# Row maxima of two attention layers: products on 32-row groups of the array, and the row of maxima written by transfer

## Reference

```python
x = x + tanh(g_xattn[0]) * attention0(layernorm(x), ctx, mask)   # 16 heads of 8
x = x + tanh(g_ffn[0])   * moe0(layernorm(x))                    # 64 experts, 8 chosen
x = x + tanh(g_xattn[1]) * attention1(layernorm(x), ctx, energy) # 16 heads of 8
x = x + tanh(g_ffn[1])   * moe1(layernorm(x))                    # 8 experts, 2 chosen
# attention: softmax(q k^T / sqrt(8)) v for each head, then the output projection;
# layer 0 masks keys, layer 1 multiplies the weights by a gate for each key
```

## Time and profile before

| | |
|---|---|
| median of 3 runs | 1072.9 us (1072.05 to 1076.41) |
| the profiled execution | 1076.31 us |
| its span | 1074.5 us |
| mean granted TensorE clock | 0.93 |
| busy: TensorE, VectorE, ScalarE, POOL | 87%, 71%, 55%, 33% of the span |
| DMA queue of SP | 86.96 MB, 34.0% of 16 engines |

### The profile page before, as it was taken

How to read it: one execution, slowest core, us unless ns; L and a number is a source line. 1 busy time by engine, 2 the same in 40 slices (tenths; PEclk the granted TensorE clock), 3 DMA queues, 4 the chain that set the end, 5 groups by cost and what they waited for, 6 DMA issues and landing times.

```text
span 1074.5 us, 24455 instructions
## 1 busy us (share of the span) xinstructions
PE 936.5 (87%) x9740; PEld 708.0 (66%) x9740; DVE 760.5 (71%) x1459; ACT 588.5 (55%) x1194; POOL 351.4 (33%) x278
## 2 busy tenths in 40 slices
PE   4589999999999989579998679999999998851996
PEld 2247677777777766468887347677777766541885
DVE  6987777676767764749997897766766765041996
ACT  2125565655565566336665227667667667621664
POOL 5800221303022110037676532243144132001774
PEclk8879999999999999679999789999999998955999
DMA  6630404134040500086652550431341340016661
GB/s 165 117 90 2 112 29 85 47 67 98 16 112 2 114 1 2 1 201 173 167 166 77 115 124 5 109 94 47 85 112 41 73 114 1 2 17 124 164 169 54
DMA packets 48088, 88.52 MB, mean 82 GB/s; under 512 B 21154, under 2 KB 31558, under 8 KB 47974
## 3 DMA queue, kind: packets, MB, share of 16 engines
q1 hardware_dynamic: 47974, 86.96, 34.0%
HBM read 47.24 MB, written 1.75 MB: 46 GB/s over the span
## 4 chain that ended last, share of the span: by engine, by line
PE 60%; DVE 15%; POOL 9%; ACT 6%; issue 5%; DMA 4%; SPq 1%; POOLq 0%; DVEq 0%; ACTq 0%
PE ps L1139 16%; PE po L1159 14%; PE pm L1110 14%; POOL tmpf L768 6%; PE ps L1142 6%; PE pc L1091 3%; PE pc L1078 3%; DVE vaug L530 3%; DVE qsel L521 3%; ACT qsel L928 3%; DMA routing<-vaug 2%; ACT probs L844 2%; POOL qbd L684 2%; DVE mx_part L412 1%; DVE junk L417 1%
## 5 line engine op out<-in xcount | busy, mean ns | idle before, releaser
L844 ACT ACTIVATE probs<-ps 121x400 f32<-121x400 f32 (+1 forms) x768 | 370.1, 505 | 236.7 <-PE ps L1142 145.1
L1139 PE MATMUL ps<-qst,kst 128*121 128x400 f32 (+1 forms) x768 | 306.3, 415 | 20.9 <-ACT probs L844 18.8
L1110 PE MATMUL pm<-khi,qbd 128*100 128x482 f32 (+1 forms) x696 | 247.4, 438 | 26.7 <-DVE mx_part L417 10.0
L412 DVE TENSOR_REDUCE mx_part<-pm 128x2 f32<-128x964 f32 (+1 forms) x160 | 178.5, 1134 | 55.2 <-PE pm L1110 55.0
L1139 PEld LDWEIGHTS ps<-qst,kst 128*121 128x121 f32 (+1 forms) x768 | 139.6, 185 | 104.2 <-ACT probs L844 61.6
L1244 PE MATMUL pm<-qsel,qst 128*128 128x400 f32 x660 | 159.5, 366 | 39.3 <-DVE qsel L521 35.4
L417 DVE CUSTOM_DVE_ANT_0 junk<-pm,negq 100x964 bf16<-100x964 f32 x128 | 148.0, 1160 | 58.4 <-PE pm L1110 58.1
L1159 PE MATMUL po<-probs,vaug 121*32 121x100 f32 x6144 | 173.7, 254 | 1.4 <-ACT probs L844 1.4
L1159 PEld LDWEIGHTS po<-probs,vaug 121*32 121x32 f32 x6144 | 130.8, 110 | 56.6 <-ACT probs L844 30.1
L1110 PEld LDWEIGHTS pm<-khi,qbd 128*100 128x100 f32 (+1 forms) x696 | 122.0, 183 | 65.4 <-DVE mx_part L417 18.8
L1244 PEld LDWEIGHTS pm<-qsel,qst 128*128 128x128 f32 x660 | 123.3, 197 | 58.4 <-DVE qsel L521 57.5
(11 more groups left out here) (176 smaller groups left out, 964.6 us busy)
## 6 DMA issues: line engine op xcount, KB each, us to landing
kst<-khi SPq DMA_DIRECT2D x128, 180.5 KB, 3.9
wb<-routing SPq DMA_DIRECT2D x66, 200.0 KB, 3.6
ctxT<-in_ctxT SPq DMA_DIRECT2D x16, 722.0 KB, 4.3
kst<-klo SPq DMA_DIRECT2D x64, 180.5 KB, 3.9
wts<-in_experts SPq DMA_DIRECT2D x55, 192.0 KB, 3.8
wb<-routing SPq DMA_DIRECT2D x22, 400.0 KB, 4.0
qsel<-qhi SPq DMA_DIRECT2D x16, 100.0 KB, 2.4
routing<-vaug SPq DMA_DIRECT2D x1, 1100.0 KB
```

The source lines that it names most:

```text
L412: nc.vector.tensor_reduce(mx_part[0:rows, i * 3 + c:i * 3 + c + len(items)], bank[:, 0:len(items), :], AX, ALU.max).then_inc(s["max_taken" ...
L844: nc.scalar.activation(probs[t % 2][0:r, g * GQ:(g + 1) * GQ], ps[0:r, n % 2, 0:GQ], ACT.Exp, scale=SCALE).then_inc(s["probs_ready"], 1)
L1110: mm = nc.tensor.matmul(pm[0:rows, n % 2 * 2 + j, 0:MAX_W], qbd[b % 2][:, first:first + rows], khi[b % 2][:, lo:lo + MAX_W], start=True, s ...
L1139: mm = nc.tensor.matmul(ps[0:r, n % 2, 0:GQ], kst[b % 2][:, g, t * KEY_TILE:t * KEY_TILE + r], qst[b % 2][:, g * GQ:(g + 1) * GQ], start=T ...
```

## The change

The maxima's products use 32 rows of the array instead of 128, each on its own group of rows (`tile_position=(32 * g, 0)`). A head's 8 features lie within 32 rows, so `qbd` shrinks to 4 x 100 columns (`head4_mask`), where the columns of `j` hold head 4g + j in row group g. Four products make a run, one into each of the four banks of `pm`; 12 runs a batch in both layers (`MAX_QUADS`). In layer 1 and for the third stretch of keys in layer 0 a run is four row groups on one stretch; for the first two stretches in layer 0 it is two row groups with two stretches each (`MAX_PAIR`). VectorE reduces banks 0 and 1, then 2 and 3, and each half frees its banks. A slot has one run, between the second score product and the value products. The first two runs of a batch stand two slots earlier: in slots 10 and 11 of the batch two before, and for batch 1 ahead of all slots. In slot 10 the parts are gathered, transposed, copied with the sign changed by ScalarE (`max_row`) into `mrow` (16 by 100), and written by one DMA from SP into row 96 of `qst`, behind the context transfer; the score products now use 97 rows and wait for that DMA. POOL makes `qbd` one batch further ahead, after the score queries.

```diff
-UNITS_PER_SLOT = [[2, 2, 2, 2, 3, 2, 2, 2, 3, 3, 1, 0], [2, 2, 2, 2, 2, 2, 2, 2, 2, 1, 1, 0]]
+MAX_QUADS = [[q for j in range(J) for q in ((MAX_PAIR, j, 0), (MAX_PAIR, j, 2), (MAX_THIRD, j, 2))],
+             [(MAX_CHUNK, j, c) for j in range(J) for c in range(3)]]
+QUADS = len(MAX_QUADS[0])
+QUADS_AHEAD = 2
+ROW_SLOT = QUADS - QUADS_AHEAD
-FIRST_K_AFTER, FIRST_K_TAKEN = [3, 7, 11], [5, 9, 13]
+FIRST_K_AFTER, FIRST_K_TAKEN = [1, 3, 5], [2, 4, 6]
...
+                def quad_max(b, k):
+                    n, (kind, j, x) = b * QUADS + k, MAX_QUADS[l][k]
...
+                    for i in range(2):
+                        bank = pm[0:S, 2 * i:2 * i + 2, 0:MAX_W]
+                        dve.wait_ge(s["chunk_ready"], 2 * n + i + 1)
+                        if kind == MAX_CHUNK:
+                            ins = nc.vector.tensor_reduce(parts[:, 2 * i:2 * i + 2, j, x], bank, AX, ALU.max)
...
                 def row_max(b):
-                    nc.vector.tensor_reduce(negm[0:rows, 96:96 + blocks], parts, AX, ALU.max)\
-                        .then_inc(s["rowmax_ready"], 1)
-                    dve.wait_ge(s["maxrow_ready"], b + 1)
-                    for lo, hi, w, off in NEGM_WRITES[l]:
-                        nc.vector.tensor_tensor(qst[b % 2][96:128, lo * rows:lo * rows + (hi - lo) * w]
...
+                    nc.vector.tensor_reduce(rowmax[:, 0:H], mx_part[0:S, :].rearrange("q (h c) -> q h c", c=3)[:, :, 0:(2, 3)[l]],
+                                            AX, ALU.max).then_inc(s["rowmax_ready"], 1)
...
                 def prep(b, par):
-                    max_queries(b)
                     score_queries(b, par)
+                    if b + 1 < B:
+                        max_queries(b + 1)
...
+                def max_row(b):
+                    act.wait_ge(s["maxrow_ready"], b + 1)
+                    if b >= 1:
+                        act.wait_ge(s["mrow_in"][(b - 1) % 2], landed(b - 1, (b - 1) % 2, 2, 16))
+                    nc.scalar.activation(mrow[:], pc[0:H, 0:S], ACT.Identity, scale=-1.0).then_inc(s["mrow_ready"], 1)
...
                         exp_group(b, t, 2)
+                        if t == ROW_SLOT and b < B - 1:
+                            max_row(b + 1)
                         exp_group(b, t, 3)
...
+                    for i, bank in enumerate((0, 2, 1, 3) if kind == MAX_PAIR else (0, 1, 2, 3)):
+                        g, c = (x + bank // 2, bank % 2) if kind == MAX_PAIR else (bank, x)
+                        lo, rows = MAX_STARTS[c], slice(32 * g, 32 * g + 32)
+                        if n >= 1 and i == 0:
+                            pe.wait_ge(s["max_taken"], 2 * n - 1)
+                        if n >= 1 and bank == 2:
+                            pe.wait_ge(s["max_taken"], 2 * n)
+                        mm = nc.tensor.matmul(pm[0:S, bank, 0:MAX_W], qbd[b % 2][rows, j * S:(j + 1) * S],
+                                              khi[b % 2][rows, lo:lo + MAX_W], start=True, stop=True,
+                                              tile_position=(32 * g, 0))
+                        if bank % 2 == 1:
+                            mm.then_inc(s["chunk_ready"], 1)
...
                         scores(b, t, 0)
-                        for u in here[0:1]:
-                            max_unit(b + 1, u)
                         scores(b, t, 1)
+                        if quad:
+                            max_quad(*quad)
                         if t >= 1:
                             weigh(b, t - 1)
                         elif b >= 1:
                             weigh(b - 1, KEY_TILES - 1)
                         scores(b, t, 2)
-                        for u in here[1:2]:
-                            max_unit(b + 1, u)
+                        if t == ROW_SLOT and b < B - 1:
+                            max_rows(b + 1)
                         scores(b, t, 3)
...
+            def row(l, b):
+                sp.wait_ge(A[l]["mrow_ready"], b + 1)
+                sp.dma_start(qst[b % 2][96:97, :].bitcast(F32),
+                             mrow[:].bitcast(F32)).then_inc(A[l]["mrow_in"][b % 2], 16)
...
+                for b in range(2, B):
+                    stack(l, b, b % 2)
+                    if b + 2 < B:
+                        context(l, b + 2, b % 2)
+                    row(l, b)
```

More of the change, by code:

```diff
@@ L199, in flamingo @@
         qst = [sb(f"qst{i}", [128, HQ], F32R) for i in range(2)]
-        qbd = [sb(f"qbd{i}", [128, HQ], F32R) for i in range(2)]
+        qbd = [sb(f"qbd{i}", [128, GQ], F32R) for i in range(2)]
         mx_part = sb("mx_part", [128, H * 3])
-        negm = sb("negm", [128, 128])
+        rowmax = sb("rowmax", [100, 128])
+        mrow = sb("mrow", [H, S], F32R)
         junk = sb("junk", [100, 2, 2, MAX_W], BF16)
@@ L394, in attention @@
             def attention(l):
-                s, units, blocks, rows = A[l], MAX_UNITS[l], MAX_BLOCKS[l], MAX_ROWS[l]
+                s = A[l]
+                parts = mx_part[0:S, :].rearrange("q (g j c) -> q g j c", j=J, c=3)
                 def k_low(b, c):
@@ L486, in attention @@
                                                     tgates[0:S, l:l + 1], xres[:], ALU.mult, ALU.add))
-                slots(-1)
+                for k in range(QUADS):
+                    quad_max(0, k)
+                    if k in FIRST_K_TAKEN:
+                        k_low(1, FIRST_K_TAKEN.index(k))
+                row_max(0)
+                for k in range(QUADS_AHEAD):
+                    quad_max(1, k)
                 slots(0)
@@ L1064, in attention @@
             def attention(l):
-                s, units, rows = A[l], MAX_UNITS[l], MAX_ROWS[l]
+                s = A[l]
                 def k_chunk(b, c):
@@ L1120, in max_rows @@
                         pe.wait_ge(s["klo_ready"], 6)
[L1121 to L1122 removed]
+                    nc.tensor.transpose(pc[:, 0:S], rowmax[:], ident[0:S, 0:S]).then_inc(s["maxrow_ready"], 1)
                 def scores(b, t, g):
@@ L1217, in slots @@
                         scores(b, t, 2)
-                        for u in here[1:2]:
-                            max_unit(b + 1, u)
+                        if t == ROW_SLOT and b < B - 1:
+                            max_rows(b + 1)
                         scores(b, t, 3)
                         beside(b, t)
-                        for u in here[2:]:
-                            max_unit(b + 1, u)
-                for u in range(len(units)):
-                    max_unit(0, u)
-                    if u in FIRST_K_AFTER:
-                        k_chunk(1, FIRST_K_AFTER.index(u))
+                for k in range(QUADS):
+                    max_quad(0, k)
+                    if k in FIRST_K_AFTER:
+                        k_chunk(1, FIRST_K_AFTER.index(k))
                 max_rows(0)
+                for k in range(QUADS_AHEAD):
+                    max_quad(1, k)
                 for b in range(B):
@@ L1406, in attention @@
                 stack(l, 1, 1)
+                row(l, 0)
                 context(l, 3, 1)
-                for i in range((B - 4) // 2):
-                    for k in range(2):
-                        stack(l, i * 2 + (2 + k), k)
-                        context(l, i * 2 + (4 + k), k)
-                stack(l, B - 2, 0)
-                stack(l, B - 1, 1)
+                row(l, 1)
+                for b in range(2, B):
[3 more added lines that the diff above has]
+                    row(l, b)
             def experts(l):
```

129 lines of the change are left out of this document (48 added, 81 removed).

## The result

| | before | after |
|---|---|---|
| median of the runs on one chip | 1073.74 us (7 runs, 1071.96 to 1077.57) | 1082.42 us (7 runs, 1079.0 to 1089.33) |
| ratio | | 1.0087, 95% interval 1.0065 to 1.0109 |
| the profiled execution | 1076.31 us, span 1074.5 | 1084.0 us, span 1082.0 |
| mean granted clock | 0.93 | 0.886 |

The kernel became 0.9% slower; 1.7% had been forecast. One of the ten executions with five spare products (1083.38 us) was slow and stands outside its ratio.

What follows compares the result with a forecast made beforehand. TensorE's stream order was taken to bound batches, VectorE the openings. Layer 0 batches -3.2, layer 1 +5.1, runs moved out -2.5, openings +15.9, row +2.8 make +18.1 us: 1091.0 us, range 1055 to 1118.

Steps and rivals of the forecast that it cites:

- E: Length of one run of maxima with its array layout change, in a slot: 0.55 us for four groups, 0.70 for pairs.
- ideal overlap: Rival, chance 0.14: row groups overlap fully, a run takes 0.42 us (four groups) or 0.64 (pairs); 1073 us, no change.
- The slot without maxima: Slot lengths without a run: 3.05 and 3.31 us in layer 0, 2.62 and 2.70 in layer 1; batches 38.5 and 32.2.
- Shade: TensorE time idle anyway, 1.26 us at a slot's end; claimed missing before the value products, so runs cost their full length.
- Openings: Before each layer's first scores: VectorE waits, more reductions in layer 1, two runs ahead of the first score; +15.9 us.
- Row transfer: Row of maxima transposed, copied and sent by DMA before a batch's first score: 0.2 us for each of 14, +2.8.
- the two runs out: Two runs of each layer move out of the slots into the openings: -2.5 us.

## Why the prediction was right, and where its sum was not

It was right with luck: errors of 33 us one way and 23 the other cancelled, and with the batches as measured and its other terms kept the sum would have said 10 us faster instead of slower. The sign, and the range of 1055 to 1118 us, held; of the 1.69% forecast 0.87% came. By its steps:

- **E.** I took 0.55 us for four groups and 0.70 for pairs; measured 0.39 and 0.62 (timelines above). This is the term that was mis-sized, and it went to what I called ideal overlap. Four weight loads did not run in sequence: they were over in 0.17 us.
- **The slot without maxima.** Layer 1: 32.2 + 12 x 0.39 = 36.9, measured 36.94, to the tenth, in part by luck: the 0.3 us in it for ScalarE's copy was not needed, and slots with k, v or the tail took as much more (up to 2.89 us without the run, where I had 2.62 and 2.70). Layer 0: 38.5 + 8 x 0.62 + 4 x 0.39 = 45.0, measured 44.1. The plain intervals from value products to value products, less E, were 2.96 to 3.00 us where I had 3.05, and those with k or v 3.23 to 3.31 where I had 3.31, and the 0.3 for the copy on ScalarE cost nothing. Batches of layer 0 below 45 us were to show the prediction wrong, and by that mark this step is: I forecast 46.3 and 38.8, that is -3.2 and +5.1 us over seven batches, and the steady difference was -2.66 and -1.13 a batch, or -18.6 and -7.9 over seven of each.
- **Shade.** My reason why the new place had to cost was that nothing waits there in vain. Moved into the shade, the runs gave back 0.4 to 0.5 us a steady batch and 1.4 to 1.7 in the batch without k products. The reading of the idle 1.26 us was right, and what fills it was not thought through: the products of k and v use the same shade today, and ScalarE's copy of v is queued ahead of the exponentials.
- **Openings.** +15.9 forecast, +14.1 measured: VectorE idles 0.82 us before a pair, as worked out from the earlier trace rows:

```profile
37.27 1.16 DVE L409 CUSTOM_DVE_ANT_0 junk<-pm,negq 100x964 bf16<-100x964 f32 x1 [0.82 <-PE pm L1114]
```

  The row transpose of layer 0 came 3.0 us later, though VectorE's first reduction came 1.5 us earlier (34.20 for 35.73), so that VectorE's part grew 4.5 us for the 5.6 forecast. The first score came 3.8 us later still (5.0 us behind the transpose for 1.16 before). Together it is 6.8 for 8.6 forecast; in layer 1 +4.5 for more reductions (5.1 forecast) and 2.8 for the first score (2.2 forecast), 7.3 for 7.3.
- **Row transfer.** I put 2.8 us; it cost nothing. The copy takes 0.23 us and the transfer, 6.2 KB, lands in 1.7 us (timeline of layer 0; landing from the view of the tile), and no wait on it is in the trace of after:

```profile
215.67 0.23 ACT L853 ACTIVATE mrow<-pc 16x100 fp32r<-16x100 f32 x1
215.92 0.52 SPq L1373 DMA_DIRECT2D qst<-mrow  x1
```

- **What my sum did not have.** First, the clock. I had read 0.78 and 0.77 in the openings and carried them over unchanged, and put nothing for the clock behind them; the opening of after is at 0.50 throughout in layer 0, and in layer 1 at 0.56 in the mean (0.50 but for its first 3 us). The first batches lost 5.3 and 6.5 us beyond their late first score and against the steady gain (layer 0: 6.5 - 3.8 + 2.66; layer 1: 8.1 - 2.8 + 1.13). That the clock makes them is shown by the spare products: 44.20 us in place of 51.94 in layer 0, and 37.31 in place of 43.96 in layer 1, with the runs behind the fourth score. The last stretch of layer 1 took 5.2 us more (180.2 for 175.0), but that is not shown to be the change's. The code there is the same in after, with the energy step late and with five spare products in the openings, and those two took:

```profile
897.40:1071.90 174.50, 123.57 (x957) 101.03 (x955) 90.55 (x166) 86.93 (x181) 57.38 (x46) 0.84 0.35 86
```

```profile
893.14:1075.50 182.36, 132.79 (x957) 107.98 (x955) 90.62 (x166) 87.09 (x181) 57.46 (x46) 0.77 0.35 83
```

  So one and the same stretch of code took 174.5 to 182.4 us in three profiled executions, longer at the lower mean clock (0.84, 0.80 and 0.77), and the kernel before, profiled once, lies within that. Second, the energy step, 4.3 us (1.6 + 2.66), shown by moving it: before, its batch was 1.5 us over a steady one, after 5.8. I had said that VectorE's reductions hide inside a slot and had not looked for other work in its queue.

Together, for the two profiled executions: batches -26.5 for +1.9, the last batch of layer 0 with its experts -2.7 (I had -2.5 for the two runs out in both layers), openings +14.1 for +15.9, row 0 for +2.8, clock +17.0 (5.2 of it in the last stretch) and energy +4.3 where I had nothing, and 1.4 more in single batches: the 7.5 us measured. So the sign and half of the size came out of a sum that was 28.6 us too dear in the batches, 4.6 too dear in openings and row, and 22.7 short of what it did not have. The first is E and the shade, the last the clock and VectorE's queue. The rival of ideal overlap had the batches nearly right and would have missed the time by about as much on the other side (1073 for 1082.4, where I had 1091).

## What to carry to other kernels

Price a filler (work put between other work, as the maxima are here) by the steady batches and, apart from that, by every stretch in which it runs alone: a form that gives TensorE less to do can lose in the clock behind it what it gains in the steady part, so read the granted clock in windows through openings and ends, not only the mean. Before a longer stretch is put down to the change, compare it among runs whose code is the same there: here such a stretch differed by 8 us. And before an order of work is judged by its batches, compare batches at the same clock. Where a product waits for all its banks, list everything else in the queue of the engine that frees them: one step of 4.6 us in it stopped all of TensorE's stream. And try a place in the stream on the longest slots first, since shade that is free in a plain slot may already be in use in one with other work.

## What the runs showed of the hardware

- Four float32 products of 32 rows by 482 columns on four row groups, with their weight loads and the change of layout, took 0.39 us of TensorE's stream; as pairs on two groups 0.62; on one group 1.04.
- The opening of layer 0 ran at 0.50 (1.2 GHz) from end to end after, with TensorE busy 22.29 of 33.46 us, and at 0.78 before, with 21.55 of 30.45; that of layer 1 at 0.56 with 18.93 of 29.72, and at 0.77 with 18.49 of 25.23. Busy time in the profile alone does not tell the clock. The 0.50 lasted until 95 us, into slots that were over 95% busy (72 to 96 us), and with five spare products of 128 rows behind each run it was gone from 40 us on. Whether the 32 rows or the shorter runs keep it low is not shown.
- In layer 1 the clock fell to 0.50 for 17 us (from 638 and from 642 us, two profiled executions) although the opening before it was at 1.00, with the runs next to the value products, and did not with the runs behind the fourth score (one). What decides this is open.
- With all four products of a run on one row group, batches of layer 1 stood at 0.50 for 14 us and more although TensorE was busy 47.28 of 48.79 us.
- A transfer of 6.2 KB into one row landed in 1.7 us (median of 16; the longest took 2.9).
